# Upper gather of a two-factor mixture of experts: rounds of both factors under one wait, two sets of four PSUM banks, x transposed in quarters

## Chip, cores and metric

One core of one Trainium2 chip runs the whole program in one launch. The metric is the device time of that core in microseconds (us). Everything is float32.

## What is computed

The reference has three stages over x (32 sequences of 64 rows, width 512): a cross attention with a context of 1601 rows, a causal self attention, and a feed-forward stage that is a mixture of 64 experts, the best two per token. Only the last one is changed:

```python
x = x + _L0_xattn_ref(_layernorm(x, axis=-1), ctx_1024, ...)
x = x + _L0_attn_ref(_layernorm(x, axis=-1), ...)
x = x + _L0_ffn_ref(_layernorm(x, axis=-1), ...)

def kmoe(x_flat, W_router, A, B, scale, bias, d_in1, d_in2, d_out1, d_out2, top_k):
    logits = x_flat @ W_router.T
    vals, idx = jax.lax.top_k(logits, top_k)
    probs = jax.nn.softmax(vals, axis=-1)
    xs = x_flat.reshape(-1, d_in1, d_in2)
    Ag = A[idx]
    Bg = B[idx]
    Y = jnp.einsum('nkoi,nij,nkpj->nkop', Ag, xs, Bg)
    out = jnp.einsum('nkop,nk->nop', Y, probs).reshape(-1, d_out1 * d_out2)
    return out * scale + bias
h = kmoe(x_flat, W_up, A_up, B_up, ...)
h = jax.nn.gelu(h, approximate=False)
y = kmoe(h, W_down, A_down, B_down, ...)
```

A token is 1024 numbers, 32 by 32; two rows of x make one token, so there are 1024 tokens, in T_N = 4 tiles of 256 (two halves t of 128). The upper layer has factors A and B of 64 by 32 for each expert, the lower one of 32 by 64.

## The kernel before, in words

The change lies in `mixture_parts` and `mixture`, and in the last quad of `self_attention`, which prepares tile 0. For each tile T the up part has two stages.

**The gather.** The factors of the chosen experts are fetched by TensorE as products of a slice of the table (weights, 64 experts by 32) with a one-hot matrix of the choices (moving, 64 by 128). It is written out by `gather_up` (line 2077): factor v (0 is A with the probabilities, 1 is B) and eight slices q of four output rows. A unit (v, q) is 4 x 4 x 2 = 32 products; each float32 product is two instructions on TensorE, so a unit is 64 instructions (line 2087), a pair of units is 128, and a tile's gather 1024. Ahead of each unit TensorE waits for the staged slice of the table (`s_ts`, a GpSimd copy into one of two buffers, `stage_table`, lines 1733 to 1737) and for the evictions of the same factor's previous unit (`s_geu`), then issues `apart`, an increment of a spare semaphore. Unit (v, q) writes PSUM banks 4v and 4v+1, so banks 0, 1, 4 and 5 are in use. ScalarE evicts the first bank of each unit (line 1976), VectorE the second (line 1813). The code on TensorE is a loop of four iterations of two slices each (lines 2211 to 2214).

**Around the gather.** TensorE waits ahead of it for the one-hots of this tile (`s_ohe["up"]`, evicted by ScalarE and VectorE at the end of the tile before, lines 1410 and 1408, from banks 2 and 3) and for the last `bias` (line 1822). The one-hots of the lower layer for tile T-1, evicted by the same lines from banks 6 and 7, are waited for only after it. Then TensorE transposes the rows of the next tile, tile T+1 (`rows`, line 1423, banks 2, 3, 6 and 7), does the lower layer's logits of tile T-1 (`logits_dn`, line 2065), the upper logits of tile T+1 (line 1430), and 16 steps of `first_up` (line 2102) and `second_up` (line 2119).

**The buffer x3s and its order.** The normalised x of one tile lies in x3s. Two readers must be through with it before SyncE loads the next tile into it: `transposed` on VectorE (line 1399), which makes xt for the steps, and `rows` of the same tile, which ran in the tile before. SyncE's order (lines 1693 to 1701) is: wait for both, load x3s for tile T+1 by two DMAs of 512 KB (line 1698), then store the four pieces of h of tile T as they come. `rows` for T+1 waits for both loads. VectorE's order in a tile is written out by hand from line 1869: for T > 0, transpose half t=0 ahead of the first eviction, and half t=1 after the evictions of q=1. For tile 0 both are done in self attention (lines 947 and 968).

**The residual of the last quad.** Its second half (`with_attended(vec, 1)`, line 787) reads bank 3, and runs on VectorE between the evictions of q=0 and q=1 of tile 0; TensorE waits for it (`rest.r2`) after the gather of tile 0, ahead of `rows`.

```python
            pe.wait_ge(s_ts, g * 2 + v + 1)
            for e in range(2):
                pe.wait_ge(s_geu[e], g * 2 + v - 1 + CREDIT)
            apart(pe, SPARE)
...
                sp.wait_ge(s_xt, 2 * T + 2)
                sp.wait_ge(s_xf, 4 * T + 4)
                for t in range(2):
                    sp.dma_start(x3s[:, t, :], x3_d[2 * T + 2 + t, :, :]).then_inc(s_x3, 16)
```

After the four tiles of the up part come four tiles of the down part, with a gather of its own (line 2159), and steps of `first_dn` (line 2133) and `second_dn` (line 2175). The change does not touch them.

## Time and profile before

| what | value |
|---|---|
| median of three timed runs | 1348.71 us (1347.95 to 1352.76) |
| the profiled execution: its own time | 1350.7 us |
| its span in the profile | 1348.9 us |
| mean granted TensorE clock | 0.968 of 2.4 GHz |
| TensorE matmul busy | 1257.8 us, 93% of the span |
| VectorE, ScalarE, GpSimd busy | 797.5, 444.7, 226.2 us |
| up part of the mixture (gather of tile 0 to the last step) | from 885 us to about 1150 us |
| down part | from about 1150 us to the end |

The profile is one execution on the chip. A timeline row gives start, length, engine, line and operation, the number of instructions merged in it, and in brackets the idle time before it with what ended it; "issue" is idle time in which the engine waited for nothing that the profile shows. PE is TensorE's matmul side, PEld its weight loads. The idle time of an engine counts only where another waits for it; as TensorE is busy nearly throughout, its pauses are what to read.

### The profile page before, as it was taken

Reading aid. Unit: us, or ns where it says so; the run is one execution under the profiler, and the core shown is the slowest. Engines: PE = TensorE matmul, PEld = TensorE weight load, DVE = VectorE, ACT = ScalarE, POOL = GpSimd, SP = SyncE. Lnnn points to the kernel's source line nnn. Section 1 sums busy time; section 2 is a strip of 40 time slices with the busy share of each in tenths; the row PEclk is TensorE's granted clock in tenths of the full one; section 3 lists DMA queues with packets and bytes.
Section 4 is the critical chain, followed back from the end, with each engine's and each line's share of the span. In section 5 each row is a group of like instructions: output and inputs, shape, how many; then the busy total and the mean of one; then the engine's idle time right before and its main releaser. Section 6 shows DMA issues by size and latency. Waiting matters only on the chain.

```text
span 1348.9 us, 61503 instructions
## 1 busy us (share of the span) xinstructions
PE 1257.8 (93%) x27944; PEld 819.2 (61%) x27944; DVE 797.5 (59%) x1489; ACT 444.7 (33%) x933; POOL 226.2 (17%) x372
## 2 busy tenths in 40 slices
PE   6999999999999999999999998887898988889886
PEld 4875333333333333676667665667787778879775
DVE  2264777677676763355555655454665746475766
ACT  0322132113112211221222212234564646454554
POOL 0000000000000001121222212114251523212212
PEclk9999999999999999999999999897999998995998
DMA  6686889998998992611011110301321205344012
GB/s 261 198 283 169 297 273 316 294 301 298 308 295 279 318 319 87 112 63 55 7 62 62 62 47 32 95 33 64 125 89 67 120 4 232 131 172 181 23 46 94
DMA packets 68082, 211.52 MB, mean 157 GB/s; under 512 B 14448, under 2 KB 30832, under 8 KB 53520
## 3 DMA queue, kind: packets, MB, share of 16 engines
q1 hardware_dynamic: 67984, 210.16, 46.0%
q8 instruction: 69, 1.13, 0.3%
q14 instruction: 29, 0.24, 0.0%
HBM read 172.37 MB, written 37.75 MB: 156 GB/s over the span
## 4 chain that ended last, share of the span: by engine, by line
PE 80%; DVE 9%; issue 5%; POOL 2%; DMA 2%; ACT 1%; SPq 1%; DVEq 0%; POOLq 0%; ACTq 0%
PE ps L686 14%; PE ps L537 10%; PE ps L1059 8%; PE ps L2133 6%; PE ps L2087 5%; DVE arena L549 5%; PE ps L234 4%; PE ps L1173 4%; PE ps L1080 4%; PE ps L2159 3%; PE ps L444 3%; PE ps L2065 2%; PE ps L2175 2%; PE ps L2102 2%; PE ps L676 2%
## 5 line engine op out<-in xcount | busy, mean ns | idle before, releaser
L549 DVE STREAM_TRANSPOSE arena<-arena 128x448 f32<-128x448 f32 (+1 forms) x512 | 263.6, 577 | 102.9 <-PE ps L537 83.7
L537 PE MATMUL ps<-arena 32*64 32x400 f32 (+1 forms) x4096 | 202.5, 506 | 0.8
L686 PE MATMUL ps<-arena 128*64 128x512 f32 x832 | 189.1, 598 | 0.0
L537 PEld LDWEIGHTS ps<-arena 32*64 32x64 f32 x4096 | 75.0, 130 | 97.5 <-issue 50.0
L686 PEld LDWEIGHTS ps<-arena 128*64 128x64 f32 x832 | 55.5, 136 | 121.4 <-issue 112.0
L570 ACT ACTIVATE arena<-ps,arena 128x384 f32<-128x384 f32 x64 | 36.3, 581 | 276.4 <-DVE arena L561 276.4
L1059 PE MATMUL ps<-arena 128*128 128x256 f32 x512 | 116.1, 385 | 0.8 <-ACT arena L994 0.8
L1059 PEld LDWEIGHTS ps<-arena 128*128 128x128 f32 x512 | 97.9, 193 | 17.8 <-issue 3.3
L1991 ACT COPY arena<-ps 128x512 f32<-128x512 f32 x128 | 75.0, 586 | 82.8 <-PE ps L2133 57.9
L1822 DVE SCALAR_TENSOR_TENSOR arena<-ps,arena 128x512 f32<-128x512 f32 x64 | 69.7, 1114 | 45.5 <-PE ps L2119 45.4
L2133 PE MATMUL ps<-arena 64*64 64x32 f32 x4096 | 83.5, 235 | 4.5 <-issue 4.3
L859 POOL TENSOR_TENSOR arena<-arena 128x1024 f32<-128x1024 f32 x8 | 18.9, 2366 | 406.4 <-PE ps L686 406.4
L2133 PEld LDWEIGHTS ps<-arena 64*64 64x64 f32 x4096 | 77.3, 152 | 8.6 <-issue 5.7
L2087 PE MATMUL ps<-arena 64*32 64x128 f32 x4096 | 70.4, 277 | 12.4 <-issue 6.4
L2087 PEld LDWEIGHTS ps<-arena 64*32 64x32 f32 x4096 | 59.6, 107 | 23.6 <-issue 19.9
L927 DVE SCALAR_TENSOR_TENSOR arena<-ps,arena 128x512 f32<-128x512 f32 x32 | 20.6, 686 | 82.0 <-PE ps L1070 82.0
L1761 POOL COPY arena<-arena 128x512 f32<-128x512 f32 x64 | 41.7, 656 | 160.8 <-ACT arena L2006 89.1
L2159 PE MATMUL ps<-arena 64*64 64x256 f32 x1024 | 62.8, 398 | 5.7 <-DVE arena L1835 3.2
L234 PE MATMUL ps<-arena 128*128 128x512 f32 x128 | 60.2, 605 | 0.0
L1813 DVE COPY arena<-ps 128x512 f32<-128x512 f32 x64 | 43.7, 690 | 27.7 <-PE ps L2087 27.6
L2159 PEld LDWEIGHTS ps<-arena 64*64 64x64 f32 x1024 | 49.5, 141 | 16.4 <-issue 10.4
L1080 PE MATMUL ps<-arena 128*64 128x256 f32 x512 | 58.8, 380 | 0.0
(145 smaller groups left out, 1850.5 us busy)
## 6 DMA issues: line engine op xcount, KB each, us to landing
arena<-ctx SPq DMA_DIRECT2D x64, 1024.0 KB
arena<-ctx SPq DMA_DIRECT2D x32, 768.0 KB
arena<-q_n SPq DMA_DIRECT2D x64, 256.0 KB, 11.4
h_n<-arena SPq DMA_DIRECT2D x16, 1024.0 KB, 4.5
arena<-h_n SPq DMA_DIRECT2D x16, 1024.0 KB, 9.5
arena<-x SPq DMA_DIRECT2D x16, 512.0 KB, 4.8
arena<-ctx SPq DMA_DIRECT2D x32, 256.0 KB
x_n<-arena SPq DMA_DIRECT2D x16, 512.0 KB, 3.5
```

What stands on the lines that cost most here:

```text
L234: x = pe.matmul(ps[:, par, :], early.ats[:, c, par::2], early.xwv[:, c, :], start=c == 0, stop=c == DC - 1)
L537: last = pe.matmul(ps[b * SEQ:(b + 1) * SEQ, tb, 0:WIDTH[tb]], qs[p % 2][r, db, b * SEQ:(b + 1) * SEQ], z[r, at % RING, b, 0:WIDTH[tb]], s ...
L549: vec.transpose(z[:, at % RING, :, g * 224:g * 224 + nt * 32].rearrange("p b (j t) -> p b j t", t=32), slots[slot_of(k)][:, :, 0:nt, db * ...
L686: last = pe.matmul(ps[b * SEQ:(b + 1) * SEQ, OB, :], probt[:, j, b * SEQ:(b + 1) * SEQ], slot[:, b, jj, :], start=j == 0, stop=j == TILES - 1)
L1059: last = pe.matmul(ps[:, bank, m % 2 * QROWS:(m % 2 + 1) * QROWS], w[n][:, c, m * P:(m + 1) * P], lnt[:, c, :], start=c == 0, stop=c == DC ...
L1080: last = pe.matmul(ps[e * SEQ:(e + 1) * SEQ, 2 + pair, s2 * 256:(s2 + 1) * 256], lnt[:, c, at:at + SEQ], w["swv"][:, c, :].rearrange("p (m ...
L1173: last = pe.matmul(ps[:, (OUT if more else LAST_OUT) + par, :], aot[:, c, par::2], w["swo"][:, c, :], start=c == 0, stop=c == DC - 1)
L1822: vec.scalar_tensor_tensor(h[:, q, :, at].rearrange("p j g -> p g j"), ps[:, b:b + 2, :].rearrange("p b (g x) -> p (b g) x", x=2 * F1)[:, ...
L1991: act.copy(mid[u].rearrange("p (b x) -> p b x", b=2), ps[:, 2 * u:2 * u + 2, 0:256]).then_inc(s_me, 1)
L2087: last = pe.matmul(ps[c * R:(c + 1) * R, 4 * v + hf, o * P:(o + 1) * P], tab_st[v][r, o, :], x, start=True, stop=True)
L2133: last = pe.matmul(ps[k * F1:(k + 1) * F1, 2 * u + t, g * D1:(g + 1) * D1], st_h[u][rows_t, g * F1:(g + 1) * F1], two(st_a[u])[rows_t, k, ...
L2159: last = pe.matmul(ps[t * E:(t + 1) * E, 2 * (g % 4) + hf, o % 2 * 2 * P:(o % 2 + 1) * 2 * P], tab_dn[v][r, o, :], x, start=True, stop=True)
```

## The change

Both factors of a slice q become one round of 128 instructions under one set of waits. Rounds alternate between two sets of four banks: `gather_bank` gives banks 2, 3, 6 and 7 for even q and 0, 1, 4 and 5 for odd q. A round waits for the evictions of the round before the last, and for both staged slices. The table is staged into two buffers for each factor, two slices ahead. As the gather now uses the banks of the choices, TensorE waits for the lower one-hots and for the last quad's residual ahead of the gather, and, ahead of `rows`, for the evictions of q=6. The second half of that residual moves on VectorE ahead of the evictions of tile 0. `transposed` does a quarter of a tile in place of a half; for T > 0 the quarters follow the evictions of q=0, 2, 4 and 6. The counts of `s_xt` double with it, on SyncE and ScalarE.

```diff
--- before.py
+++ after.py
@@ -944,7 +944,8 @@
                     vec.reciprocal(rden[n], den[n]).then_inc(S["rd"], 1)
             if not more:
                 first.fold_of(vec)
-                first.transposed(vec, 0, 0)
+                first.transposed(vec, 0, 0, 0)
+                first.transposed(vec, 0, 0, 1)
             done(vec, "pt", q * ITEMS + 4)
             vec.tensor_copy(pt[3], ps[:, 5, :].rearrange("p (h t) -> p h t", h=HPC)).then_inc(S["pte_d"], 1)
             if not more:
@@ -965,7 +966,8 @@
                 first.weights_of(vec, "up", 0)
                 first.weigh(vec, "up", 0)
                 first.one_hot_out(vec, "up", 0, 1, 1)
-                first.transposed(vec, 0, 1)
+                first.transposed(vec, 0, 1, 0)
+                first.transposed(vec, 0, 1, 1)
                 with_attended(vec, q, u, 0, LAST_OUT)
         vec.wait_ge(early.s_pv, TILES * (PAIRS - 1))
         front(0, 0)
@@ -1235,7 +1237,7 @@
     wr_dn = wr_at.rearrange("p (o e) -> p o e", e=E)
     y = tables["up_at"].rearrange("p (t r b) -> p t r b", t=2, r=R)
     x2b, yt = (wr_at[:, u * 4 * D:(u + 1) * 4 * D].rearrange("p (t f) -> p t f", t=2) for u in range(2))
-    tab_st = [area(4, D1) for _ in range(2)]
+    tab_st = [[area(4, D1) for _ in range(2)] for _ in range(2)]
     hb_at = top_area.at
     xft = top_area(2, 8, P)
     ohx_up, oht_up = top_area(2, 4, P), top_area(2, 4, 2, E)
@@ -1293,10 +1295,14 @@
     UP = STEPS * T_N
+    def gather_bank(v, q):
+        return 4 * v + 2 * ((q + 1) % 2)
     def gathered_up(v, q, hf):
         dst = fac[v].rearrange("p (m o) -> p m o", o=F1)[:, :, 32 * hf + 4 * q:32 * hf + 4 * q + 4]
-        return dst, ps[:, 4 * v + hf, :].rearrange("p (o m) -> p m o", o=4)
+        return dst, ps[:, gather_bank(v, q) + hf, :].rearrange("p (o m) -> p m o", o=4)
     def gathered_dn(v, g):
@@ -1392,12 +1398,13 @@
                           prob[k].rearrange("p t k -> p (t k)").unsqueeze(2).unsqueeze(3).to_broadcast([P, 4, 2, E]),
                           ALU.mult).then_inc(s_ohp[k], 1)
-    def transposed(vec, T, t):
+    def transposed(vec, T, t, half):
         vec.wait_ge(s_x3, 32 * T + 32)
         if T:
             vec.wait_ge(s_stx, STEPS * T + AHEAD)
-        vec.transpose(xt[:, t, :, :].rearrange("p r j -> p j r"),
-                      x3s[:, t, :].rearrange("n (i j) -> n j i", j=D1)).then_inc(s_xt, 1)
+        js = slice(half * D1 // 2, (half + 1) * D1 // 2)
+        vec.transpose(xt[:, t, :, js].rearrange("p r j -> p j r"),
+                      x3s[:, t, :].rearrange("n (i j) -> n j i", j=D1)[:, js, :]).then_inc(s_xt, 1)
     def one_hot_out(e, k, i, part, bank):
@@ -1692,7 +1700,7 @@
         for T in range(T_N):
             if T + 1 < T_N:
-                sp.wait_ge(s_xt, 2 * T + 2)
+                sp.wait_ge(s_xt, 4 * T + 4)
                 sp.wait_ge(s_xf, 4 * T + 4)
                 for t in range(2):
                     sp.dma_start(x3s[:, t, :], x3_d[2 * T + 2 + t, :, :]).then_inc(s_x3, 16)
@@ -1732,9 +1740,9 @@
         def stage_table(T, q):
             for v in range(2):
-                if T or q:
-                    pool.wait_ge(s_gu, 16 * T + 2 * (q - 1) + v + 1)
-                pool.tensor_copy(tab_st[v], tab_up[v][:, 4 * q:4 * q + 4, :]).then_inc(s_ts, 1)
+                if T or q >= 2:
+                    pool.wait_ge(s_gu, 16 * T + 2 * (q - 2) + v + 1)
+                pool.tensor_copy(tab_st[q % 2][v], tab_up[v][:, 4 * q:4 * q + 4, :]).then_inc(s_ts, 1)
         def stage_a(T, n):
             if n == 0:
@@ -1771,11 +1779,13 @@
         pool.sem_inc(s_sta, AHEAD)
         pool.sem_inc(s_stb, AHEAD)
         pool.memset(euler, EULER).then_inc(s_fold, 1)
+        pool.sem_inc(s_ts, CREDIT - 4)
         stage_table(0, 0)
+        stage_table(0, 1)
         pool.wait_ge(s_fold, 2)
         exponential("up", 0)
         for T in range(T_N):
-            for q in range(1, 8):
+            for q in range(2, 8):
                 stage_table(T, q)
             stage_a(T, 0)
             stage_a(T, 1)
@@ -1791,6 +1801,7 @@
                     rest.rstd(pool)
             if T + 1 < T_N:
                 stage_table(T + 1, 0)
+                stage_table(T + 1, 1)
         for T in range(T_N):
             for n in range(STEPS):
                 stage_b_dn(T, n)
@@ -1867,16 +1878,14 @@
         vec.sem_inc(s_sth, UP + AHEAD - 2)
         vec.sem_inc(s_ohe["dn"][1], CREDIT)
         for T in range(T_N):
-            if T:
-                transposed(vec, T, 0)
+            if T == 0:
+                rest.with_attended(vec, 1)
             for q in range(8):
                 for v in range(2):
                     gather_out(T, q, v)
-                if T and q == 1:
-                    transposed(vec, T, 1)
+                if T and q in (0, 2, 4, 6):
+                    transposed(vec, T, q // 4, q // 2 % 2)
                 if T == 0:
-                    if q == 0:
-                        rest.with_attended(vec, 1)
                     if q == 2:
                         rest.with_output_bias(vec, 0)
                     if q == 4:
@@ -1977,7 +1986,7 @@
         def stage_x(T, n):
             if n == 0:
-                act.wait_ge(s_xt, 2 * T + 2)
+                act.wait_ge(s_xt, 4 * T + 4)
             if T or n >= 2:
                 act.wait_ge(s_s1, STEPS * T + n - 1)
             act.copy(st_h[n % 2][:, 0:P].rearrange("p (t x) -> p t x", t=2),
@@ -2073,20 +2082,22 @@
                 last = pe.matmul(ps[:, bank, t * E:(t + 1) * E], part[:, t, :], fold, start=True, stop=True)
             last.then_inc(s_lgb, 1)
-        def gather_up(v, g):
-            pe.wait_ge(s_ts, g * 2 + v + 1)
+        def gather_up(g, q):
+            pe.wait_ge(s_ts, g * 2 + 2 + CREDIT - 4)
             for e in range(2):
-                pe.wait_ge(s_geu[e], g * 2 + v - 1 + CREDIT)
+                pe.wait_ge(s_geu[e], g * 2 + 2 + CREDIT - 4)
             apart(pe, SPARE)
-            for o in range(4):
-                for c in range(C):
-                    for hf in range(2):
-                        r = slice(hf * E, (hf + 1) * E)
-                        x = ohx_up[r, 0, :, c * R:(c + 1) * R] if v == 0 else ohx_b[r, c % 2, c // 2]
-                        last = pe.matmul(ps[c * R:(c + 1) * R, 4 * v + hf, o * P:(o + 1) * P],
-                                         tab_st[v][r, o, :], x, start=True, stop=True)
-            last.then_inc(s_gu, 1)
+            for v in range(2):
+                for o in range(4):
+                    for c in range(C):
+                        for hf in range(2):
+                            r = slice(hf * E, (hf + 1) * E)
+                            x = ohx_up[r, 0, :, c * R:(c + 1) * R] if v == 0 else ohx_b[r, c % 2, c // 2]
+                            last = pe.matmul(ps[c * R:(c + 1) * R, gather_bank(v, q) + hf, o * P:(o + 1) * P],
+                                             tab_st[q % 2][v][r, o, :], x, start=True, stop=True)
+                last.then_inc(s_gu, 1)
         def first_up(n, u):
@@ -2203,19 +2214,22 @@
         pe.wait_ge(early.s_t, 14 * 16)
         pe.wait_ge(s_fold, 2)
+        pe.wait_ge(rest.r2, rest.r2_all)
         with pe.Fori(0, T_N) as T:
             for e in range(2):
                 pe.wait_ge(s_ohe["up"][e], T + 1)
             pe.wait_ge(s_bias, T * STEPS + CREDIT)
             apart(pe, SPARE)
+            for e in range(2):
+                pe.wait_ge(s_ohe["dn"][e], T - 1 + CREDIT)
+            apart(pe, SPARE)
             with pe.Fori(T * 4, T * 4 + 4) as j:
                 for r in range(2):
-                    gather_up(0, j * 2 + r)
-                    gather_up(1, j * 2 + r)
+                    gather_up(j * 2 + r, r)
             for e in range(2):
-                pe.wait_ge(s_ohe["dn"][e], T - 1 + CREDIT)
+                pe.wait_ge(s_geu[e], T * 16 + 14 + CREDIT)
+            apart(pe, SPARE)
             with pe.If(T < T_N - 1):
-                pe.wait_ge(rest.r2, rest.r2_all)
                 for t in range(2):
                     rows(pe, T + 1, t, ROW_BANKS[2 * t:2 * t + 2])
             for e in range(2):
```

## Rows read from the trace of the kernel before

**Rows 1.** Costliest groups of the page: busy, mean ns of one, idle before and its releaser.
```profile
L2087 PE MATMUL ps<-arena 64*32 64x128 f32 x4096 | 70.4, 277 | 12.4 <-issue 6.4 <-DVE arena L1813 3.1 <-DVE arena L1408 1.5
...
L2087 PEld LDWEIGHTS ps<-arena 64*32 64x32 f32 x4096 | 59.6, 107 | 23.6 <-issue 19.9
```
**Rows 2.** Timeline of PE, tile 1 (start, length, line, count, idle before).
```profile
952.96 4.25 PE L2087 MATMUL ps<-arena 64*32 64x128 f32 x256 [1.50 <-DVE arena L1408]
...
960.71 2.18 PE L2087 MATMUL ps<-arena 64*32 64x128 f32 x128 [1.03 <-DVE arena L1813]
963.16 4.26 PE L2087 MATMUL ps<-arena 64*32 64x128 f32 x256 [0.27 <-issue]
...
972.22 1.96 PE L1423 MATMUL ps<-arena 128*128 128x128 f32 x16 [0.26 <-issue]
```
**Rows 3.** Timeline of PE, tile 2.
```profile
1014.35 2.18 PE L2087 MATMUL ps<-arena 64*32 64x128 f32 x128 [0.22 <-issue]
1017.22 2.21 PE L2087 MATMUL ps<-arena 64*32 64x128 f32 x128 [0.69 <-ACT arena L1976]
...
1022.92 2.21 PE L2087 MATMUL ps<-arena 64*32 64x128 f32 x128 [1.03 <-DVE arena L1813]
...
1034.56 1.96 PE L1423 MATMUL ps<-arena 128*128 128x128 f32 x16 [0.30 <-issue]
```
**Rows 4.** Timelines of DVE and ACT at the start of tile 2.
```profile
1014.34 2.23 DVE L1399 STREAM_TRANSPOSE arena<-arena 128x1024 f32<-128x1024 f32 x1
...
1014.16 0.59 ACT L1410 COPY arena<-ps 128x512 f32<-128x512 f32 x1 [0.36 <-PE ps L1438]
```
**Rows 5.** Timeline of tile 3, PE and DVE: first products, last evictions, what follows.
```profile
1076.74 2.17 PE L2087 MATMUL ps<-arena 64*32 64x128 f32 x128 [0.22 <-issue]
...
1094.59 0.69 DVE L1813 COPY arena<-ps 128x512 f32<-128x512 f32 x1 [0.34 <-PE ps L2087]
...
1096.69 0.69 DVE L1813 COPY arena<-ps 128x512 f32<-128x512 f32 x1 [0.37 <-PE ps L2087]
...
1097.78 7.27 PE L2065 MATMUL ps<-arena 64*64 64x128 f32 x256 [1.15 <-DVE arena L1813]
```
**Rows 6.** Timeline of weight loads (PEld), tile 3: two units.
```profile
1086.33 0.91 PEld L2087 LDWEIGHTS ps<-arena 64*32 64x32 f32 x64 [0.15 <-issue]
...
1092.32 2.98 PEld L2087 LDWEIGHTS ps<-arena 64*32 64x32 f32 x192 [0.52 <-issue]
```
**Rows 7.** Timeline of SP, then half a microsecond by windows (last: clock, DMA share, GB/s).
```profile
1022.30 0.81 SPq L1698 DMA_DIRECT2D arena<-x_n  x2
...
1026.00:1026.50 0.50, 0.50 (x48) 0.38 (x37) 0.00 (x0) 0.00 (x0) 0.00 (x0) 1.00 0.15 57
```
**Rows 8.** Timelines of tile 0: PE, and DVE with the last quad's residual.
```profile
885.15 2.77 PE L2087 MATMUL ps<-arena 64*32 64x128 f32 x157
890.76 7.30 PE L2087 MATMUL ps<-arena 64*32 64x128 f32 x355 [2.84 <-issue]
...
888.03 0.68 DVE L787 TENSOR_TENSOR arena<-ps,arena 128x512 f32<-128x512 f32 x1
```
**Rows 9.** Timeline of PE: first work after two other pauses.
```profile
848.01 1.97 PE L1423 MATMUL ps<-arena 128*128 128x128 f32 x8 [9.00 <-DMA arena<-x_n]
...
912.53 1.11 PE L1430 MATMUL ps<-arena 128*128 128x64 f32 x4 [3.14 <-issue]
```
**Rows 10.** Windows: length, busy PE, PEld, DVE, ACT, POOL, then granted clock, DMA share, GB/s.
```profile
848.00:853.50 5.50, 5.49 (x17) 4.78 (x18) 0.00 (x0) 1.17 (x2) 0.00 (x0) 0.50 0.98 209
...
891.00:894.50 3.50, 3.50 (x146) 3.33 (x138) 1.38 (x2) 1.19 (x2) 0.59 (x2) 0.52 0.02 5
...
915.30:925.20 9.90, 9.86 (x220) 9.52 (x219) 0.65 (x1) 2.03 (x6) 2.34 (x4) 0.50 0.01 3
```
**Rows 11.** The same view in the down part: steps of tile 1, steps of tile 2.
```profile
1215.40:1247.60 32.20, 31.99 (x1252) 30.20 (x1249) 16.17 (x28) 13.98 (x26) 9.47 (x15) 0.50 0.48 188
...
1277.00:1293.00 16.00, 14.12 (x912) 13.21 (x913) 11.21 (x21) 9.43 (x17) 6.34 (x10) 1.00 0.34 132
```

More of the change, by code:

```diff
@@ L1544, in mixture_parts @@
     f.gathered_dn = gathered_dn
+    f.gather_bank = gather_bank
     f.unit_done = unit_done
@@ L1650, in mixture @@
     UP = first.UP
-    gathered_up = first.gathered_up
+    gathered_up, gather_bank = first.gathered_up, first.gather_bank
     gathered_dn = first.gathered_dn
```

## Prediction

> **What bounds the kernel now.** I read first the costliest groups, to see how much of TensorE's time the gather is: 70.4 us busy, with 12.4 us of idle time in front of its products, 6.4 of it "issue", 3.1 on VectorE's evictions and 1.5 on VectorE's one-hots [rows 1]. That is small beside a span of 1348.9 us, so the question is what each pause is, tile by tile. Next, TensorE's timeline. Let s be the start of a tile's gather. In tile 1, s is 952.96 and the next stage (`rows`) starts at 972.22, s+19.26 [rows 2]. In tile 2 it is 1014.35 to 1034.56, 20.21 [rows 3]. In tile 3, where no `rows` follows, the lower logits start at 1097.78, 21.04 after 1076.74 [rows 5]. An undisturbed loop iteration (four units, 256 instructions) is 4.27 us and 0.27 to the next [rows 2], 4.54 in all. The reader is to see the pauses on top: 1.03 in tile 1 [rows 2], 0.69 and 1.03 in tile 2 [rows 3]; tile 3 repeats tile 2. The name beside the 0.69 is ScalarE, but VectorE began a transposition of 2.23 us at 1014.34 [rows 4], so the first eviction came only after it. The weight loads show something finer: 0.91 us for the 64 of a unit, then 0.15 us of "issue" at the boundary of two units, 0.52 at the end of an iteration [rows 6].
>
> **Part 1, no waits between the factors.** Eight boundaries a tile go. Their price is not shown without the waits. Lower bound 0, if the bubble is the change of operands. Upper bound: a unit's 64 loads at the spacing inside it, (0.91-0.11)/63 x 64 = 0.81 us, 0.11 being the length of one load [rows 1, 6], against two units in 2.10 us of evictions (1094.59 to 1096.69 [rows 5]), 1.05 each, that is 0.24. I take the visible 0.15 [rows 6]: 1.2 us a tile. An iteration becomes 4.54-0.30 = 4.24.
>
> **Part 2, two sets of banks and quarters.** The 1.03 of tile 1 and the 1.72 of tiles 2 and 3 go. A quarter moves 512 elements where 1024 took 2.23 [rows 4]; half is 1.1. In an iteration VectorE then has four copies of 0.69 and one quarter, 3.9 of 4.24 us, with a round in reserve, so it keeps up. Nothing is late next inside the gather. GpSimd stages two rounds ahead of use and costs nothing; without that cover it would be its own copy. The DVE copy after q=6 does delay the last two evictions, below.
>
> **Part 3, earlier waits.** In tiles 2 and 3 the gather now waits for the lower one-hots: of the two copies ScalarE's ends last, at 1014.75 [rows 4]; with 0.1 to wake TensorE that is 1014.85 in place of 1014.35, +0.5 each. Tile 1 has no lower one-hots. In tile 0 it waits for the last quad's residual, 0.68 us on VectorE [rows 8], which can only start when the projection ends, where the gather began before, 885.15 [rows 8]; with the way to VectorE and back: +0.85, and -1.2 from part 1, so -0.35. The 2.84 us pause in tile 0, called "issue" [rows 8], I leave as it is; if its cause is a thing that comes at a fixed time, the later start is absorbed and up to 0.85 more is won, and if it vanishes, with its slow products, some 4. Two transpositions as four in self attention: +0.1.
>
> **Part 4, the load of x3s: the step that decides.** The load of tile T+1 may start only when all of tile T's transpositions are done, and `rows` of T+1 waits for it. Before, the second half ended early: SyncE issued at 1022.30, eight microseconds into the gather, and the DMA engines were through at about 1026.2 (a share of 0.15 in the half microsecond from 1026.0) [rows 7]; `rows` came at 1034.56, so the load was hidden. After, the last quarter stands behind q=6. Three iterations are 12.72. The second eviction of an iteration starts 2.24 in (1094.59 [rows 5], with products from 1092.35, 0.03 behind the iteration's first load [rows 6]), less one boundary: 2.09. So s+14.81, copy 0.69, quarter 1.1: s+16.6. Load 3.9 from issue to end [rows 7]: s+20.5, and 0.1 to wake: s+20.6. TensorE ends its last round at 12.72+3.97 = s+16.7 and then idles 3.9 us. Against before: tile 1 20.6-19.26 = +1.35; tile 2 20.6+0.5-20.21 = +0.9. The load of tile 0 starts long before its gather ends, and tile 3 has none. The queue behind the loads on SyncE, the four stores of h, waits for gelu much later: nothing. For the range I allow the load 3.5 to 4.5.
>
> Tile 3: the quarter ends at s+16.6, two copies follow (the last eviction started at 1096.69 with TensorE ready for it [rows 5], now VectorE is behind): s+17.9; the 0.4 from there to the logits [rows 5]: 18.3, plus 0.5: 18.8 against 21.04, -2.2.
>
> **Part 5, TensorE's clock.** Three pauses in rows: 2.84 us [rows 8], 3.14 and 9.00 us [rows 9]. After each the granted clock is half (1.2 GHz, against 2.4): for 3.5 us of work from 891.0, for 5.5 us from 848.0, and for 9.9 us from 915.3 [rows 10]. The two new pauses of 3.9 us are longer than the shortest of these, so I expect the same. What then runs is bound by the array: 8 transpositions take 1.97 us at half clock [rows 9], 16 take 1.96 at full [rows 3], exactly twice. So the loss is half the slow time: 1.75 by the shortest stretch, 4.9 by the longest, 0 if the clock holds. I take 2.25, between the stretches of 3.5 and 5.5, whose work (dense products, or the same transpositions first) is nearest. Two of them: +4.5.
>
> **Sum.** -0.35 +0.1 +1.35 +0.9 -2.2 +4.5 = +4.3 us. On the profiled execution's own 1350.7 that is 1355.0; that execution lies 2.0 above the median 1348.7, so for the median 1353.0. A measurement of this kernel can tell about 0.5%, 6.7 us, from no change.
>
> **The rivals.**
>
> Slower: the clock stays low through the transpositions. The mechanism is that `rows`, the first work after the pause, doesn't bring the clock back: in the stretch from 848.0 the clock stayed at half through the 1.97 us of transpositions and the products behind them until 853.5. If the 3.9 us of `rows` at half clock do not count, and 3.5 us of logits at half clock follow, the loss is 1.95+1.75 = 3.7 each, up to the 4.9 of the longest row. Sum +4.3+2.9 = +7.2: 1355.9 (1358.3 with 4.9). It decides from 3.5 us lost at each pause. The Trainium skill, "TensorE: Matmul & The Clock Gate", Part 4: PE-mode transpose, says that transpose-mode work isn't counted as busy in the same way; by that rule this rival is the case, and the row from 848.0 does not contradict it, though it can't separate the two readings. The same page, HAM oscillation, speaks against the change as such: a wait for a transfer between bursts of products makes each next burst start cold. The rows agree after 2.84, 3.14 and 9.00 us.
>
> The clock holds. Against it stand all three pauses. +4.3-4.5 = -0.2: 1348.5.
>
> The boundaries cost the same without their waits: 7 x 0.15 back in tiles 1 and 2, 8 x 0.15 in 0 and 3, +4.5: 1357.5. For it: nothing shows a boundary without waits; against it: inside a unit the loads show no bubble.
>
> The load is hidden after all. Then tiles 1 and 2 gain 2.2 and 2.7, with no clock loss: -7.3: 1341.4. Against it stand SyncE's wait for all transpositions and the 3.9 us.
>
> The down part's clock changes hands. From 1215.4 to 1247.6 tile 1's steps ran at half clock, 38.9 instructions a microsecond against 57.0 in tile 2's at full [rows 11]: 32.2 x (1-38.9/57.0) = 10.2 us, and with the gather behind it about 12. No long pause preceded it, so it hangs on small things, and this change shifts all that follows it. Gone: +4.3-12, 1341.0. A second one: +16, 1365. For its staying: three timed runs lie within 4.8 us, less than this price, so each has about as much of it.
>
> **How the numbers follow.** Forecast 0.47; clock low through the transpositions 0.18; clock holds 0.07; boundaries unchanged 0.07; load hidden 0.03; down stretch gone 0.10; a second one 0.08. The likeliest case alone spans 1349 to 1357 (load 3.5 to 4.5, boundary 0 to 0.24, clock 1.75 to 2.75, tile 0). The range reaches to the slower rival and into the faster ones: 1343 to 1360. Slower by over 6.7 us: most of the slower rival and of the boundary case, the second stretch, and a tail of the forecast: 0.30. Faster by as much: most of the stretch gone and of the hidden load: 0.12. Within: 0.58.
>
> **What would show it.** Part 1: 128 weight loads in a row without the 0.15. Part 2: no pause on VectorE's evictions. Part 3: tile 2's first product 0.1 after ScalarE's one-hot copy. Part 4: in tiles 1 and 2 a pause of about 3.9 us in front of `rows`, released by the DMA, its issue about 16.6 after s. Part 5: half clock for some 3.5 to 5.5 us behind it. Wrong: a hidden load, or a pause under 2.5 us.

## The result, and the profile after

The changed kernel takes 1355.07 us (median of 15 runs, 1352.66 to 1357.78) against 1348.79 us before (15 runs): a ratio of 1.0049, 95% interval 1.0036 to 1.0061. It is slower by 6.3 us. The two profiled executions took 1353.96 us (span 1352.1) and 1350.7 us (span 1348.9), which is 3.3 us apart.

TensorE's timeline of tile 1 in the changed kernel, to be read beside [rows 2] (line 2098 is the gather, 1430 `rows`, 2074 the lower logits):

```profile
949.32 3.95 PE L2098 MATMUL ps<-arena 64*32 64x128 f32 x256 [1.77 <-issue]
953.61 3.96 PE L2098 MATMUL ps<-arena 64*32 64x128 f32 x256 [0.33 <-issue]
957.85 3.95 PE L2098 MATMUL ps<-arena 64*32 64x128 f32 x256 [0.29 <-issue]
962.10 3.95 PE L2098 MATMUL ps<-arena 64*32 64x128 f32 x256 [0.29 <-issue]
970.67 3.68 PE L1430 MATMUL ps<-arena 128*128 128x128 f32 x16 [4.62 <-DMA arena<-x_n]
974.28 8.20 PE L2074 MATMUL ps<-arena 64*64 64x128 f32 x256
```

The gather runs without a pause, in 3.95 us an iteration where 4.27 stood, and then TensorE waits 4.62 us for the load. Who made the load late is in the timelines of VectorE and SyncE in the same tile:

```profile
964.17 0.69 DVE L1824 COPY arena<-ps 128x512 f32<-128x512 f32 x1 [0.18 <-PE ps L2098]
964.78 1.25 DVE L1406 STREAM_TRANSPOSE arena<-arena 128x512 f32<-128x512 f32 x1
...
966.09 0.81 SPq L1706 DMA_DIRECT2D arena<-x_n  x2
```

The last quarter ends at 966.03, SyncE issues the load 0.06 later, and the first row transposition comes 4.58 us after that. The DMA engines are busy until about 970.1 (a share of 0.22 from 970.0 to 970.2, none behind it), so 4.0 us of the 4.58 are the transfer and some 0.6 the way from its end to TensorE's first product. The weight loads of the same tile show what became of the boundary of [rows 6]. There are now 128 loads in a row, and 0.15 us of "issue" stands only between two rounds:

```profile
957.82 1.78 PEld L2098 LDWEIGHTS ps<-arena 64*32 64x32 f32 x128 [0.53 <-issue]
959.75 1.78 PEld L2098 LDWEIGHTS ps<-arena 64*32 64x32 f32 x128 [0.15 <-issue]
```

The rows of tile 2 and tile 3 that answer to [rows 3, 5]:

```profile
1016.63 3.96 PE L2098 MATMUL ps<-arena 64*32 64x128 f32 x256 [1.33 <-ACT arena L1417]
...
1038.02 3.45 PE L1430 MATMUL ps<-arena 128*128 128x128 f32 x16 [4.69 <-DMA arena<-x_n]
...
1082.84 3.95 PE L2098 MATMUL ps<-arena 64*32 64x128 f32 x256 [1.33 <-ACT arena L1417]
...
1101.03 7.29 PE L2074 MATMUL ps<-arena 64*64 64x128 f32 x256 [1.49 <-DVE arena L1824]
```

The granted clock behind the two pauses is the third number from the end of each window:

```profile
969.20:976.20 7.00, 5.53 (x52) 5.20 (x56) 0.00 (x0) 2.34 (x4) 0.00 (x0) 0.52 0.12 47
976.20:982.00 5.80, 5.80 (x220) 5.80 (x216) 0.00 (x0) 0.00 (x0) 0.00 (x0) 1.00 0.00 0
1037.50:1041.30 3.80, 3.28 (x16) 3.22 (x16) 0.00 (x0) 1.59 (x3) 0.00 (x0) 0.55 0.00 0
```

Laid side by side from the last product of self attention to the end (885.22 before, 882.81 after), the two traces differ by 5.6 us. That last product ended 2.4 us earlier in the changed kernel's profile, which is why the two spans differ by only 3.2 us. In nine profiles of kernels that all have the change's code up to there it ended between 882.8 and 890.1, so the 2.4 us can't be put down to the change. The stages:

| stage | before | after | difference |
|---|---|---|---|
| tile 0: end of projection to `rows` | 22.21 | 20.86 | -1.35 |
| tile 0: `rows` to first step | 13.86 | 12.53 | -1.33 |
| tile 0: steps, to gather of tile 1 | 31.67 | 33.12 | +1.45 |
| tile 1: gather to `rows` | 19.26 | 21.35 | +2.09 |
| tile 1: `rows` to gather of tile 2 | 42.13 | 45.96 | +3.83 |
| tile 2: gather to `rows` | 20.21 | 21.39 | +1.18 |
| tile 2: `rows` to gather of tile 3 | 42.18 | 44.82 | +2.64 |
| tile 3: gather to logits | 21.04 | 18.19 | -2.85 |
| the rest | 251.12 | 251.07 | -0.05 |

Two rows need a second look. In tile 0 the gather begins later and pauses longer than before, and is shorter all the same:

```profile
884.96 2.63 PE L2098 MATMUL ps<-arena 64*32 64x128 f32 x157 [2.15 <-issue]
888.92 1.72 PE L2098 MATMUL ps<-arena 64*32 64x128 f32 x99 [1.33 <-issue]
```

Both kernels pause behind the same 157 instructions, for 2.84 us before [rows 8] and for 1.33 now, and 2.15 us of waiting are new ahead of the gather. What shrank is the products' own time, from 18.60 to 16.22 us: some 1.2 us for the boundaries, and about as much because the clock stayed at full speed from 888.9 to 895, where before it had been halved for 3.5 us behind the pause. The rows "`rows` to gather of tile 2" and "of tile 3" hold the slow work behind each pause (2.65 and 1.49 us) and the later start of the next gather (1.11 us each).

### The profile page after: what moved, and what is told of

It reads as the page before. It is cut to its first block, busy times and chain, and to the rows that moved or that the text cites. A ratio compares the mean times of both kernels' runs of the same rounds, so it can differ in the third digit from the quotient of the medians.

```text
span 1352.1 us, 61430 instructions
## 1 busy us (share of the span) xinstructions
PE 1255.2 (93%) x27944; PEld 816.8 (60%) x27944; DVE 797.2 (59%) x1497; ACT 445.7 (33%) x933; POOL 225.8 (17%) x372
## 3 DMA queue, kind: packets, MB, share of 16 engines
q8 instruction: 69, 1.13, 0.3%
## 4 chain that ended last, share of the span: by engine, by line
PE 81%; DVE 9%; issue 4%; POOL 2%; DMA 2%; ACT 1%; SPq 0%; DVEq 0%; POOLq 0%; ACTq 0%
PE ps L686 14%; PE ps L537 10%; PE ps L1061 8%; PE ps L2144 6%; DVE arena L549 5%; PE ps L234 4%; PE ps L444 4%; PE ps L1175 4%; PE ps L2098 4%; PE ps L1082 4%; PE ps L2170 3%; PE ps L2074 2%; PE ps L2113 2%; PE ps L2186 2%; PE ps L676 2%
## 5 line engine op out<-in xcount | busy, mean ns | idle before, releaser
L1061 PE MATMUL ps<-arena 128*128 128x256 f32 x512 | 114.9, 382 | 0.8 <-ACT arena L996 0.8
L2144 PEld LDWEIGHTS ps<-arena 64*64 64x64 f32 x4096 | 77.6, 153 | 8.8 <-issue 5.8
L2098 PE MATMUL ps<-arena 64*32 64x128 f32 x4096 | 63.7, 271 | 11.4 <-issue 8.2
L234 PE MATMUL ps<-arena 128*128 128x512 f32 x128 | 60.2, 605 | 0.0
L1175 PE MATMUL ps<-arena 128*128 128x512 f32 x128 | 57.8, 593 | 0.8 <-ACT arena L1037 0.8
L444 PE MATMUL ps<-arena 128*128 128x256 f32 x256 | 58.3, 379 | 0.0
```

Of the source, the lines that this page charges most:

```text
L234: x = pe.matmul(ps[:, par, :], early.ats[:, c, par::2], early.xwv[:, c, :], start=c == 0, stop=c == DC - 1)
L444: last = pe.matmul(ps[:, QB + h, m % 2 * QROWS:(m % 2 + 1) * QROWS], wqk[:, c, m * P:(m + 1) * P], lnt[n][:, c, :], start=c == 0, stop=c = ...
L1061: last = pe.matmul(ps[:, bank, m % 2 * QROWS:(m % 2 + 1) * QROWS], w[n][:, c, m * P:(m + 1) * P], lnt[:, c, :], start=c == 0, stop=c == DC ...
L1175: last = pe.matmul(ps[:, (OUT if more else LAST_OUT) + par, :], aot[:, c, par::2], w["swo"][:, c, :], start=c == 0, stop=c == DC - 1)
L2098: last = pe.matmul(ps[c * R:(c + 1) * R, gather_bank(v, q) + hf, o * P:(o + 1) * P], tab_st[q % 2][v][r, o, :], x, start=True, stop=True)
L2144: last = pe.matmul(ps[k * F1:(k + 1) * F1, 2 * u + t, g * D1:(g + 1) * D1], st_h[u][rows_t, g * F1:(g + 1) * F1], two(st_a[u])[rows_t, k, ...
```

## The experiments

Each ratio compares a run with runs of the kernel before on the same chip, and has its 95% interval. Runs on different chips are best compared by these ratios: the kernel before took 1348.8 us beside the change, and 1349.6 to 1351.2 us beside the experiments.

**The place of the last transposition, in the changed kernel.** The first run moves the quarters:

```diff
-                if T and q in (0, 2, 4, 6):
-                    transposed(vec, T, q // 4, q // 2 % 2)
+                if T and q in (0, 1, 2, 3):
+                    transposed(vec, T, (0, 1, 2, 3).index(q) // 2, (0, 1, 2, 3).index(q) % 2)
```

> The changed kernel with its quarters of x after q=0, 1, 2 and 3 in place of 0, 2, 4 and 6; nothing else differs. Theory (the late load of x3s is the loss): the last quarter ends some 9 us into the gather, the load is through by 14, rows follows the last product by 0.3 us in place of 4.6 and 4.7, and the clock stays at 1.0 there. That returns 2 x 4.3 us of pause and 4.1 us of slow work (2.6 in tile 1, 1.5 in tile 2): 1355.1 - 12.7 = 1342.4 us, ratio to before 0.995. Rival (the loss is elsewhere: the one-hot wait, the banks, the code): at most 2 us come back, 1353 us.

Measured: 1341.3 us, ratio 0.9939 (0.9920 to 0.9958). That is 8.6 us less than the kernel before on the same chip, where the change took 6.3 more on its own: 15 us between them, 13.8 by the bare medians, and 12.7 expected. `rows` follows the gather at once, at full clock:

```profile
952.67 3.95 PE L2098 MATMUL ps<-arena 64*32 64x128 f32 x256 [1.77 <-issue]
...
969.73 1.96 PE L1430 MATMUL ps<-arena 128*128 128x128 f32 x16 [0.33 <-issue]
```

The rival falls: four numbers in a tuple decide between slower and faster. One of the seven timed runs took 1354.9 us, and the profile caught that one; its two slow stretches are shown under "The down part" below. The same profile shows something that the theory did not ask for, in tile 3:

```profile
1073.36 5.38 PE L2098 MATMUL ps<-arena 64*32 64x128 f32 x256 [1.33 <-ACT arena L1417]
```

Here the first iteration took 5.38 us and not 3.95, behind the pause of 1.33 us that the one-hot wait makes. The granted clock was 0.50 from 1073.3 to 1075.0. In the seven kernels of this document that have a pause of 1.32 to 1.85 us ahead of the gathers of tiles 1 to 3 because of the new waits, 4 of 21 such gathers begin so, for 1.4 us each. None of 15 does in the five kernels that have no such waits ahead of the gather, where the pause is 0.2 us in tiles 2 and 3 and 1.5 in tile 1. So the earlier waits can cost more than their pause, in some executions and not in others.

**The same with quarters after q=0, 2, 4 and 5.**

> The changed kernel with quarters after q=0, 2, 4 and 5. The last one ends one round, 2.1 us, earlier, so the pause ahead of rows shrinks from 4.6 to about 2.5 us in tiles 1 and 2. Theory A (a pause of 2.5 us still halves the clock, as 2.8 us did in tile 0 of the kernel before): only 4.2 us come back, 1350.9 us, with half clock behind rows. Theory B (it is too short for that): 4.1 us more come back, 1346.8 us, clock 1.0 there.

Measured: 1349.5 us, ratio 0.9998 (0.9983 to 1.0013). Two pauses of nearly one length had different ends, in tile 1 and in tile 2:

```profile
975.04 1.97 PE L1430 MATMUL ps<-arena 128*128 128x128 f32 x16 [2.52 <-DMA arena<-x_n]
...
1018.26 5.42 PE L2098 MATMUL ps<-arena 64*32 64x128 f32 x256 [1.32 <-ACT arena L1417]
...
1039.01 3.48 PE L1430 MATMUL ps<-arena 128*128 128x128 f32 x16 [2.56 <-DMA arena<-x_n]
```

After 2.52 us the clock held, after 2.56 it was halved (3.48 us where 1.96 is full speed). The products just ahead were the same and at full clock in both tiles; the first iteration of tile 2's gather, some 15 us earlier, had been at half clock (5.42 us), that of tile 1 not. So neither theory holds as put: in this kernel a pause of this length goes either way. The pause shrank as foretold. The profile is of the fastest of the twelve executions, 1342.2 us.

**The kernel before with the late half alone.**

```diff
-                if T and q == 1:
+                if T and q == 6:
                     transposed(vec, T, 1)
```

> The kernel before with one thing moved: the transposition of half t=1 stands behind the evictions of q=6, not of q=1. Units, banks and waits are those of before. Theory (the place of the last transposition alone makes the loss): the half ends 2.2 us after the eviction of q=6, the load needs 4.4 us more, rows waits for it some 5 us in tiles 1 and 2, and the clock falls as in the changed kernel: +3.9 +3.9 +0.6 +4.2 = +12.6, 1361.4 us, with the pause of 1.03 us in each tile gone. Rival (it takes the new rounds or banks to lose time): within 2 us of 1348.8.

Measured: 1364.8 us, ratio 1.0096 (1.0069 to 1.0123), four runs; 13.6 us more than the kernel before on that chip, 12.6 expected. Tile 1:

```profile
976.26 3.67 PE L1423 MATMUL ps<-arena 128*128 128x128 f32 x16 [5.35 <-DMA arena<-x_n]
```

The pause is there without any new round, bank or wait, 5.35 and 5.34 us in tiles 1 and 2, with slow rows in both. The place of the last transposition is enough for the loss. The profiled execution was the slowest of the four, 1374.4 us; its down part has two long stretches at half clock (below), so its total is no measure, and only its rows are read here.

**Other work in the place of the pause.** The lower logits go ahead of `rows`; ahead of both TensorE waits for the evictions of q=7. The main lines of the edit:

```diff
+            for e in range(2):
+                pe.wait_ge(s_geu[e], T * 16 + 16 + CREDIT)
+            with pe.If(T > 0):
...
+                logits_dn(0)
             with pe.If(T < T_N - 1):
                 for t in range(2):
                     rows(pe, T + 1, t, ROW_BANKS[2 * t:2 * t + 2])
-            with pe.If(T > 0):
...
-                logits_dn(0)
```

> The changed kernel, quarters as it has them, with the lower logits of tile T-1 issued on TensorE ahead of rows of tile T+1, not behind it. Theory (TensorE idles in rows because the load is late, so any other work may stand there): in tiles 1 and 2 the 7.3 us of logits cover the load; they wait for the last two evictions, as in tile 3, some 1.5 us. Pause 1.5 in place of 4.6, clock kept: 1355.1 - 2 x 3.1 - 4.1 = 1344.8 us. Rival (the load is held up by something that follows rows or by its queue): the pause moves behind the logits and stays near 4 us, 1353 us.

Measured: 1349.2 us, ratio 0.9984 (0.9967 to 1.0000), 2.0 us less than the kernel before on that chip. Against the change that is some 8.5 us back by the ratios and 5.9 by the bare medians, where 10.3 were expected; the times alone can't rule the expectation out. The rows show where it fell short. In the profiles 4.5 us come back between the gather and the first step in tiles 1 and 2, and 1.0 is lost in tile 0. Tile 1:

```profile
974.43 7.27 PE L2074 MATMUL ps<-arena 64*64 64x128 f32 x256 [1.52 <-DVE arena L1824]
981.63 1.97 PE L1430 MATMUL ps<-arena 128*128 128x128 f32 x16
984.65 5.13 PE L1437 MATMUL ps<-arena 128*128 128x64 f32 x32 [1.06 <-ACT arena L1424]
```

The load is hidden and its pause gone. But the upper logits (line 1437) need ScalarE's copies of the transposed rows, which the lower logits had covered: 1.06 us of new wait, and they took 5.13 us in place of 3.79, with the clock at 0.70 on average from 984 to 991. Tile 2 shows the same (1.06 and 5.32 us). So the clock fell behind a pause of only 1.06 us that stood behind 1.97 us of transpositions. In tile 0, where no lower logits are there to fill the place, `rows` now waits for the last evictions too; it pauses for 4.74 us, called "issue", and runs at half clock (3.52 us). The expectation had not asked what the moved work had been hiding.

**What the clock costs: products nobody reads in the pause.** Four products of 128x512, in tiles 0 to 2, change nothing that is computed.

```diff
             with pe.If(T < T_N - 1):
+                for _ in range(4):
+                    pe.matmul(ps[:, 2, :], first.xft[:, 0, 4, :], first.xft[:, 0, 0:4, :].rearrange("p c n -> p (c n)"), start=True, stop=True)
                 for t in range(2):
```

> The changed kernel with four products of 128x128 by 128x512 (3.7 us) that nobody reads, ahead of rows in tiles 0, 1 and 2; in tiles 1 and 2 they fill the pause in which TensorE waits for x3s. Theory (rows and the logits behind it are slow because the pause halves the clock): rows takes 1.96 us in tiles 1 and 2, the logits 7.3, 4.1 us come back, and tile 0 pays 3.7: 1355.1 + 3.7 - 4.1 = 1354.7 us. Rival (rows is slow for another reason, such as reading x3s just loaded): rows stays at 3.4 to 3.7 us, 1358.8 us.

Measured: 1356.95 us, ratio 1.0054 (1.0033 to 1.0075). Tile 2 (line 2234 is the filler):

```profile
1039.41 3.69 PE L2234 MATMUL ps<-arena 128*128 128x512 f32 x8 [0.20 <-issue]
1043.77 1.97 PE L1430 MATMUL ps<-arena 128*128 128x128 f32 x16 [0.67 <-DMA arena<-x_n]
1045.67 7.27 PE L2074 MATMUL ps<-arena 64*64 64x128 f32 x256
```

In both tiles `rows` is back at 1.96 us and the logits at 7.27, though x3s is as freshly loaded as before: the slow work was the clock's. The total lies 2.2 us above the expectation, and 1.3 above it if both are taken against the kernel before on the same chip, which is within the interval. Part of it is in tile 0: from the gather to the first step it took 4.8 us more and not 3.7, with a pause of 4.95 us ahead of the upper logits.

**What a satisfied wait costs.** On top of the early quarters:

```diff
             for v in range(2):
+                if v:
+                    pe.wait_ge(s_ts, g * 2 + 2 + CREDIT - 4)
+                    for e in range(2):
+                        pe.wait_ge(s_geu[e], g * 2 + 2 + CREDIT - 4)
+                    apart(pe, SPARE)
```

> The kernel with the early quarters (after q=0, 1, 2, 3), and between the two factors of a round the same three waits and the spare increment as ahead of a round; all of them are long satisfied. Theory (the 0.15 us at a boundary is the price of the waits and the increment): 0.15 back at 32 boundaries, +4.8 us, about 1347.2 us, iterations of 4.27 us in place of 3.96 and 0.15 of issue after each 64 weight loads. Rival (it comes with the change of operands, or is hidden): no change, 1342.4 us.

Measured: 1346.8 us, ratio 0.9982 (0.9968 to 0.9997), 5.5 us over the kernel without them. In tile 2 the gather takes 17.85 us against 17.03, so 0.82 for eight boundaries, 0.10 each and not 0.15:

```profile
1013.44 4.12 PE L2103 MATMUL ps<-arena 64*32 64x128 f32 x256 [1.33 <-ACT arena L1417]
1017.91 4.13 PE L2103 MATMUL ps<-arena 64*32 64x128 f32 x256 [0.35 <-issue]
```

The sign is right; four tiles of 0.82 explain 3.3 of the 5.5 us. Tile 1's first iteration took 5.51 us in that profile, with the clock halved (1.4 us), but the profile of the kernel without the waits has such an iteration too, in tile 3, so the other 2.2 us stay open. From start to start an iteration fell from 4.54 to 4.25 us, 0.145 a boundary, of which the waits explain 0.10. The other 0.04 may come from the new bank order or elsewhere; no run separates them.

**Are quarters needed?** Two runs answer this. One has the change with halves at their old places; another has the kernel before with quarters after q=0 to 3.

```diff
+            else:
+                transposed(vec, T, 0)
             for q in range(8):
...
-                if T and q in (0, 2, 4, 6):
-                    transposed(vec, T, q // 4, q // 2 % 2)
+                if T and q == 1:
+                    transposed(vec, T, 1)
```

> The changed kernel with halves of x in place of quarters, where the kernel before has them: one ahead of the first eviction, one after q=1. Rounds, banks and waits stay those of the change. Theory (two sets of banks alone take up the 2.2 us transpositions; the quarters are not needed): no pause inside the gather, load hidden, as fast as the early quarters, 1341.3 us. Rival (a half still stops TensorE, since it is longer than a round of 2 us): up to 1 us a tile in tiles 1 to 3, 1344.3 us.

```diff
-                if T and q == 1:
-                    transposed(vec, T, 1)
+                if T and q < 4:
+                    transposed(vec, T, q // 2, q % 2)
```

> The kernel before with quarters of x after q=0, 1, 2 and 3; units, banks and waits are those of before. Theory (the merged rounds give about 1.3 us a tile and the early quarters the rest): the pauses of 0.69 and 1.03 shrink to some 0.3 each quarter, 1.0 to 1.7 us come back in tiles 1 to 3 in part, 1346 us, and the weight loads still show 0.15 at each unit. Rival (quarters give nothing without a second set of banks, since a quarter of 1.2 us is longer than the slack of a unit): four pauses of 0.5 us or more a tile, 1348.8 us.

Measured: 1342.3 us, ratio 0.9940 (0.9921 to 0.9959) for the halves, and tiles 1 and 2 take 17.02 us each, as with early quarters: two sets of banks take up a transposition of 2.2 us, and cutting it buys nothing that these runs can show. The quarters in the old kernel give 1347.7 us, ratio 0.9990 (0.9974 to 1.0007), which can't be told from no change, though tile 2's gather is 18.67 us in place of 20.21, with 0.51 and 0.28 us of pause left.

**The late one-hot wait.** The two bank sets are swapped, so that the early waits move from ahead of round 0 to ahead of round 1; `rows` and the lower logits change banks with it.

```diff
-        return 4 * v + 2 * ((q + 1) % 2)
+        return 4 * v + 2 * (q % 2)
...
-    ROW_BANKS = (2, 3, 6, 7)
+    ROW_BANKS = (0, 1, 4, 5)
...
-                parts(T, 0)
+                parts(T, 2)
...
                 for r in range(2):
+                    if r:
+                        pe.wait_ge(rest.r2, rest.r2_all)
+                        for e in range(2):
+                            pe.wait_ge(s_ohe["dn"][e], T - 1 + CREDIT)
+                        apart(pe, SPARE)
                     gather_up(j * 2 + r, r)
...
-                logits_dn(0)
+                logits_dn(2)
```

> The kernel with the early quarters, and the two sets of banks swapped: even rounds use banks 0, 1, 4 and 5, so the waits for the lower one-hots and for the last quad's residual move from ahead of round 0 to ahead of round 1; rows of the next tile go to banks 0, 1, 4 and 5 and the lower logits to banks 2 and 3. Theory (the wait ahead of the gather costs 1.1 us in tiles 2 and 3, 0.5 for the one-hot and the rest for restarting, and 0.9 to 2.2 in tile 0): 1342.4 - 2.2 - 1.5 = 1338.7 us, tile 2's first product 0.2 to 0.3 us after the transposed choices in place of 1.33. Rival (the time to restart is that of the loop's end and remains): 1341.4 us.

Measured: 1344.5 us, ratio 0.9957 (0.9942 to 0.9972). The median is 3.2 us above that of the early quarters, not below it; the two intervals overlap slightly, and the rows agree with the medians. Tile 2 starts 0.24 us behind the choices, as foretold, but its gather takes 18.05 us: each odd round now has 0.42 us of idle weight-load time in front of it where 0.15 stood, four times a tile. So the waits were taken out of the loop by peeling rounds 0 and 7 off, and the loop runs three times over two rounds in place of four times:

```diff
+            gather_up(T * 8, 0)
+            pe.wait_ge(rest.r2, rest.r2_all)
+            for e in range(2):
+                pe.wait_ge(s_ohe["dn"][e], T - 1 + CREDIT)
+            apart(pe, SPARE)
+            with pe.Fori(T * 4, T * 4 + 3) as j:
+                for r in range(1, 3):
+                    gather_up(j * 2 + r, r % 2)
+            gather_up(T * 8 + 7, 1)
```

> The kernel with swapped banks, with round 0 and round 7 outside the loop and three iterations of rounds (1,2), (3,4), (5,6): the waits for the lower one-hots and the residual are issued once in a tile and not in each iteration. In the kernel with swapped banks they stretched the gap between two rounds from 0.15 to 0.42 us, four times a tile. Theory (a satisfied wait costs issue time wherever it stands): 4 x 0.27 us a tile and one loop end (0.4 us) come back, 1344.5 - 4.3 - 1.5 = 1338.7 us, tile 2's gather 16.6 us long in place of 18.05. Rival (twice the code has to be fetched): the first pass in tile 0 loses 2 us and more, 1341 to 1343 us.

Measured: 1370.3 us, ratio 1.0166 (1.0138 to 1.0194). Both theories fall; the rival had named code that must be fetched, but only for the first pass. Here are tile 1's gather, and the page's row of the instruction queue (packets, MB, share):

```profile
956.23 0.67 PE L2098 MATMUL ps<-arena 64*32 64x128 f32 x32 [3.49 <-issue]
961.41 5.64 PE L2098 MATMUL ps<-arena 64*32 64x128 f32 x252 [4.51 <-issue]
968.67 1.72 PE L2098 MATMUL ps<-arena 64*32 64x128 f32 x100 [1.62 <-issue]
```

```profile
q8 instruction: 101, 1.65, 0.5%
```

The gathers of tiles 1 to 3 have three pauses of "issue" each, of 1.3 to 4.5 us, 22.3 us in all, and 101 packets of instructions are fetched in place of 69, 1.65 MB in place of 1.13. The tile loop's body grew by two rounds; it seems no longer to be kept from one tile to the next. That the pauses are those fetches isn't shown: no row ties a packet to a pause. The other way to free TensorE from these waits is to let GpSimd wait, ahead of the table of round 1:

```diff
                 stage_table(T + 1, 0)
+                for e in range(2):
+                    pool.wait_ge(s_ohe["dn"][e], T + CREDIT)
                 stage_table(T + 1, 1)
```

> The kernel with swapped banks and early quarters, with the waits for the lower one-hots and the residual taken off TensorE: GpSimd waits for them before it stages the table of round 1, for which TensorE waits in any case. Theory (the satisfied waits in the loop cost 0.27 us in each of 16 iterations, and the wait ahead of the gather 1.1 us in tiles 2 and 3): both are gone, tile 2's gather 17.0 us with its first product 0.24 us behind the choices, 1344.5 - 4.3 = 1340.2, and 2 us under the kernel with early quarters in the same state of the down part, 1339 to 1340 us. Rival (GpSimd stages round 1 too late, behind the one-hot): a pause of 0.5 us or more between rounds 0 and 1, 1342 us.

Measured: 1340.3 us, ratio 0.9936 (0.9915 to 0.9956), the lowest median of all. Tile 2:

```profile
1012.91 3.95 PE L2101 MATMUL ps<-arena 64*32 64x128 f32 x256 [0.23 <-issue]
...
1029.94 1.96 PE L1430 MATMUL ps<-arena 128*128 128x128 f32 x16 [0.33 <-issue]
```

Both costs are gone and no pause replaces them. Against the early quarters (1341.3) the intervals overlap, so its lead over them isn't shown by the times, only by the rows. Against the swapped banks with the waits on TensorE (1344.5) it is 4.2 us, as expected, and the intervals overlap there too (0.9956 against 0.9942).

**The down part.** The profile of the early quarters has two long stretches at half clock there (25 us or more), that of the quarters up to q=5 none; the kernel before has one [rows 11]. In this order:

```profile
1220.00:1247.00 27.00, 26.58 (x936) 23.89 (x940) 11.09 (x21) 10.68 (x19) 5.54 (x9) 0.50 0.54 214
1271.00:1301.00 30.00, 29.16 (x1030) 26.39 (x1034) 12.39 (x24) 11.03 (x19) 6.39 (x10) 0.50 0.18 70
```

```profile
1215.00:1250.00 35.00, 30.11 (x1587) 27.24 (x1591) 22.65 (x35) 21.03 (x35) 12.84 (x18) 1.00 0.46 181
1260.00:1300.00 40.00, 33.87 (x1627) 29.73 (x1628) 28.29 (x40) 24.43 (x40) 12.85 (x18) 1.00 0.14 52
```

The two executions took 1354.9 and 1342.2 us, 13.6 above and 7.3 below the medians of their kernels. The kernel code of that part is the same in both. What a stretch costs can be read off the traces, from the lower logits of tile 3 to the end: 238.8 us with no such stretch, 248.5 to 251.7 in the ten profiles with one, the kernel before and the changed one among them (251.1 each), and 260.4 and 263.2 in the two with two (the early quarters, and the late half in the old kernel). So a stretch costs some 10 to 13 us. What starts or ends it is open.

## Why the prediction was right

**Right.** 1353.0 was predicted and 1355.07 measured, inside the range; the measured +6.3 us is just under the 6.7 us taken as the bound. The deciding step, part 4, held: the last quarter ended at s+16.7 (16.6 predicted), and `rows` waited for the DMA in tiles 1 and 2. The early quarters and the late half in the old kernel show it from both sides. Part 5 held as well: there is half clock behind both pauses, and the filler removes it.

**Sizes, term by term.**
- Part 1: 0.29 us less an iteration (4.54 to 4.25), 0.30 predicted. But the waits as its reason are shown only for 0.10 of each 0.145.
- Part 2: no pause on evictions worth counting is left; a quarter took 1.2 us, not 1.1. What the prediction did not see is that two sets of banks alone do this, so that the quarters, whose last one made the loss by its place, were not needed.
- Part 3: the start of tiles 2 and 3 came 1.11 us later, not 0.5. ScalarE's copy ended at 1015.92 and the first product began at 1016.63, 0.71 after it and not 0.1. No row of the prediction shows 0.1 for a wait ahead of the gather, and tile 1 before had shown more (one-hot at 952.11, first product at 952.96). In tile 0 the wait for the residual cost 2.15 us, not 0.85: the residual ended at 883.53, and the first product began 1.43 after it. In tile 1, which the prediction left as it was, the added waits move the first product from 1.50 to 1.77 us behind the choices.
- Part 4: the pause was 4.62 and 4.69 us, not 3.9. The transfer took 4.0 us, nearly the 3.9 predicted; from its end to the first transposition 0.6 passed, not 0.1. So tile 1 gave +2.09 us for +1.35, and tile 2, with the later start of part 3, +2.29 for +0.9.
- Tile 3: its gather to the logits is 2.85 us shorter; with the 1.11 of the later start that leaves -1.7, where -2.2 was predicted.
- Part 5: `rows` and the logits lost 2.65 us in tile 1 and 1.49 in tile 2, 4.14 together against 4.5. The clock came back at 976.3 and 1041.3; the second is at the end of the transpositions themselves, so they didn't prevent the recovery there. The rival that it stays low through them, and the Trainium skill's rule behind it ("TensorE: Matmul & The Clock Gate", Part 4: PE-mode transpose), fits tile 1 in part (8.20 us of logits in place of 7.27) and not tile 2. The experiment with the logits first speaks a little for it: there the clock fell behind 1.97 us of transpositions and 1.06 of pause. No run settles it. A wait for a transfer does make the next burst start cold, as the Trainium skill says in the same page's section on HAM oscillation: in both tiles here at 4.6 us, and in one of two at 2.5.
- Tile 0: -1.35 in the gather, -0.35 predicted. The pauses grew there by 0.64 us (2.15 and 1.33 in place of 2.84), and the clock that held behind the shorter one made up for it; the prediction had named such a case, but with the pause gone as well. Up to the first step -1.33 more came, all of it from two pauses called "issue" (2.80 and 0.71 in place of 3.14 and 1.70), and the prediction had nothing for them. What causes these pauses is open. +1.45 followed in the steps behind them: 0.27 is the wait ahead of the gather of tile 1, and most of the rest half clock from 935.3 to about 938.3, behind a pause of 1.78 us, where one of 1.81 before had left the clock at full.

**The terms together.** They sum to +5.6 us by the traces, where +4.3 was predicted: the pauses and late starts of tiles 1 to 3 were forecast 2.6 us too short, the gain in tile 0 0.9 too small and the loss to the clock 0.4 too large. These errors cancel in part, which is luck; so is it that the change left the number of slow stretches in the down part alone.

The rivals that fell: hidden load, clock holding, boundaries at full cost. The one on the down part is real as a mechanism, seen both ways in the experiments. It doesn't carry the result: the profiles before and after have one stretch each and take 251.1 us there, and the 15 runs of the changed kernel lie within 5.1 us.

## What to carry to other kernels

When work is cut finer and spread to smooth one engine, follow its last piece: who may start only after it, and how long that takes. Here the last quarter sat on the release of a buffer whose reload feeds TensorE. A place in a list turned a gain of 8.6 us into a loss of 6.3. And give a wait to an engine with idle time, if TensorE already waits for that engine: a group of satisfied waits that a loop passed 16 times cost TensorE 4 us a run, and peeling the loop to avoid it cost 26.

## What the runs showed of the hardware that was not expected

- A loop body that grows by two rounds (512 instructions with their weight loads) made TensorE pause for "issue" in every tile, for 22.3 us in nine pauses in tiles 1 to 3, with 101 instruction packets in place of 69.
- A satisfied wait is not free on TensorE: three and an increment cost 0.10 us between the two factors of a round, and as many cost 0.27 where a round's own waits stood already. Why the two differ is open.
- Two pauses of 2.52 and 2.56 us, with the same work just ahead and behind, ended one at full and one at half clock.
- Pauses of 1.32 to 1.85 us ahead of the gather, behind short transpositions, were followed by half clock in 4 of 21 cases, for 1.4 us each.
- From the end of a wait outside the loop to TensorE's first product 0.71 us passed in tiles 2 and 3, and 1.43 in tile 0.
- A stretch of some 30 us at half clock in the same code can be there once, twice or not at all, worth some 10 to 13 us each time. The total of one profile is then no measure of a kernel; a median of many runs is a better one.
